# A burst of gathers opens after six of eight landings, and three one-hot tables are gathered from the second block on

## What is computed

```python
e = jnp.stack([tbl_0[ids[:, 0]], ..., tbl_25[ids[:, 25]]], axis=1)      # (2048, 26, 128)
combined = jnp.concatenate([sparse_x, dense_x[:, None, :]], axis=1)     # 27 features
interact = jnp.einsum('bfd,bgd->bfg', combined, combined)
z = interact[:, _TRIU_I, _TRIU_J]                                       # 351 pairs
h = jnp.concatenate([z, r_dense_x], axis=1)
h = jnp.maximum(h @ W_top1 + b_top1, 0.0)                               # 479 -> 512
h = jnp.maximum(h @ W_top2 + b_top2, 0.0)                               # 512 -> 256
y = h @ W_top3                                                          # 256 -> 1
```

## Time and profile before

| | us |
|---|---|
| median of 3 runs | 430.12 |
| lowest, highest | 429.4, 431.53 |
| span of the profiled execution | 427.9 |
| PE busy | 405.9 (95%) |
| POOL busy | 274.3 (64%) |
| ACT busy | 264.6 (62%) |
| DVE busy | 207.0 (48%) |

### The profile page before, as it was taken

One profiled execution on the slowest core, in us unless ns is written; L12 is line 12 of the kernel. 1 busy time (PEld: TensorE's weight loads), 2 busy tenths in 40 slices (PEclk: granted clock), 3 DMA queues, 4 the chain that ended last, 5 costly groups with the idle time before them and its releaser, 6 DMA issues.

```text
span 427.9 us, 8390 instructions
## 1 busy us (share of the span) xinstructions
PE 405.9 (95%) x3220; PEld 380.9 (89%) x3220; DVE 207.0 (48%) x238; ACT 264.6 (62%) x926; POOL 274.3 (64%) x292
## 2 busy tenths in 40 slices
PE   3898999999999989998999989999999989999997
PEld 2787899899999979998999989998899989989886
DVE  5788868441467134751367224661348324621142
ACT  3343477867675657657575756756576665766642
POOL 6557877766777667767776677766777676666000
PEclk9999999999999999999999999999999999999999
DMA  6776333312112121213112121212112121111000
GB/s 179 221 223 182 88 108 98 100 50 87 51 51 74 51 82 49 75 51 87 50 51 75 48 84 51 74 44 87 49 51 75 51 86 50 49 47 51 12 3 2
DMA packets 18073, 32.06 MB, mean 75 GB/s; under 512 B 5928, under 2 KB 8880, under 8 KB 18032
## 3 DMA queue, kind: packets, MB, share of 16 engines
q0 software_dynamic: 9088, 18.63, 15.6%
q1 hardware_dynamic: 8064, 12.08, 9.1%
q10 hardware_dynamic: 880, 0.80, 0.6%
HBM read 31.48 MB, written 0.01 MB: 74 GB/s over the span
## 4 chain that ended last, share of the span: by engine, by line
PE 82%; ACT 8%; DMA 7%; DVE 1%; issue 1%; ACTq 0%; SPq 0%
PE x_ps L612 29%; PE gram_ps L628 26%; PE tail_ps L683 12%; DMA hot_in<-in_tbl 7%; PE x_ps L593 6%; ACT gram L410 4%; PE tail_ps L660 3%; PE tail_ps L652 3%; PE tail_ps L689 2%; ACT h_hi L443 1%; ACT h L444 1%; ACT xt L386 1%; PE x_ps L720 1%; DVE onehot L873 0%; PE tail_ps L731 0%
## 5 line engine op out<-in xcount | busy, mean ns | idle before, releaser
L576 POOL DMA_INDIRECT raw<-in_tbl,ids_sb x284 | 273.4, 963 | 121.6 <-issue 74.0
L873 DVE TENSOR_TENSOR onehot<-ids_wide,row_ps 128x1024 fp32r<-128x1024 int16 (+1 forms) x142 | 163.6, 1181 | 103.7 <-PE x_ps L612 101.8
L410 ACT COPY gram<-gram_ps 32x104 f32<-32x104 f32 x496 | 117.4, 237 | 49.9 <-PE gram_ps L628 43.4
L612 PE MATMUL x_ps<-onehot,hot_hi 128*128 128x256 f32 x496 | 130.7, 298 | 10.0 <-ACT xt L386 9.6
L628 PE MATMUL gram_ps<-xt 128*128 128x108 f32 x1024 | 129.3, 276 | 2.1 <-ACT xt L820 0.8
L628 PEld LDWEIGHTS gram_ps<-xt 128*128 128x128 f32 x1024 | 122.1, 191 | 5.3 <-ACT gram L410 1.3
L612 PE MATMUL x_ps<-onehot,hot_lo 128*128 128x256 f32 x496 | 122.6, 281 | 0.0
L612 PEld LDWEIGHTS x_ps<-onehot,hot_hi 128*128 128x128 f32 x496 | 93.5, 188 | 15.8 <-ACT xt L386 11.4
L612 PEld LDWEIGHTS x_ps<-onehot,hot_lo 128*128 128x128 f32 x496 | 93.6, 189 | 0.0
L386 ACT COPY xt<-x_ps 128x128 f32<-128x128 f32 (+1 forms) x90 | 40.8, 509 | 42.7 <-PE x_ps L612 42.3
L820 ACT COPY xt<-x_ps 128x512 f32<-128x512 f32 (+1 forms) x78 | 44.2, 622 | 1.3 <-PE x_ps L593 1.3
(11 more groups left out here) (76 smaller groups left out, 317.0 us busy)
## 6 DMA issues: line engine op xcount, KB each, us to landing
raw<-in_tbl,ids_sb POOLq DMA_INDIRECT x284, 2.5
ids_wide<-in_hot_ids SPq DMA_DIRECT2D x16, 256.0 KB, 3.4
hot_in<-in_tbl SPq DMA_DIRECT2D x14, 256.0 KB, 3.3
hot_in<-in_tbl SPq DMA_DIRECT2D x6, 320.0 KB, 3.5
weights_in_place<-in_w SPq DMA_DIRECT2D x10, 128.0 KB, 2.2
dense_sb<-in_dense_t ACTq DMA_DIRECT2D x6, 128.0 KB, 2.4
dense_sb<-in_dense_t SPq DMA_DIRECT2D x2, 128.0 KB, 3.7
w1d_sb<-in_w SPq DMA_DIRECT2D x2, 128.0 KB
```

The source lines that it names most:

```text
L410: last = copy(gram[rows, :, per_fill * i:per_fill * (i + 1)], src)
L576: nc.gpsimd.indirect_dma_start(out=raw[k][:, f, :], out_offset=None, in_=sources[f], in_offset=bass.IndirectOffsetOnAxis(ap=ids_sb[:, t, f ...
L612: last = nc.tensor.matmul(ps, table[:, chunk_at[j] + c, :], moving[:, c - a, :], start=(c == 0 and table is tables_of[0]), stop=(c == chun ...
L873: nc.vector.tensor_tensor(columns(p), ids_wide[:, it // IDS % IDS_RING, it % IDS, 0:width].unsqueeze(1).to_broadcast([P, n, width]), row_n ...
```

## The change

`SHARES` becomes 3 from block 1 on, so that `MOST` is 3: the three tables of 10 chunks are all gathered there, and the seven tables of 8 chunks stay items. `raw` and `ids_sb` grow by one feature. The turns of a later tile take 19 gathers, still in five groups (3, 4, 4, 4, 4 in place of 3, 4, 3, 4, 4). Through `block_orders` the direct tables of block 0 become the items 0, 2, 4, 6, 7, 8 and 9 in place of 0, 2, 4, 6, 8 and 9. `BURST_OPEN = 2`: the wait ahead of a burst leaves out the last two gathers of the burst before, and both count on `last_in`.

```diff
-SHARES = (0, 2, 2, 2, 2, 2, 2, 2)
+SHARES = (0, 3, 3, 3, 3, 3, 3, 3)
 MOST = max(SHARES)
@@
 BURST = 8
+BURST_OPEN = 2
@@
     def is_last(t, f):
-        return gather_no[t, f] % BURST == BURST - 1
+        return gather_no[t, f] % BURST >= BURST - BURST_OPEN
@@
         def burst_landed(eng, k):
 
-            last_of = {(t, group_of[t, f]): f for t, f in gathers[k * BURST:(k + 1) * BURST - 1]}
+            last_of = {(t, group_of[t, f]): f for t, f in gathers[k * BURST:(k + 1) * BURST - BURST_OPEN]}
             for (t, g), f in last_of.items():
                 eng.wait_ge(lead_in[t % RAW][g], landed(t, g, False, f))
```

## The result

The changed kernel takes 417.0 us (median of 4 runs, 415.3 to 417.31) against 430.82 for the kernel before beside it (429.4 to 432.33): a ratio of 0.9656 (95% interval 0.9621 to 0.969). It is faster, by 3.1 to 3.8%. The forecast was 414.8. The profiled execution spans 415.5 us, where the prediction had 412.6.

What follows compares the result with a forecast made beforehand. PE bounds, POOL just under it: 427.9 - 16.45 - 0.45 + 1.4 = 412.4 us, a few tenths for their meeting give 412.6 profiled; the median, 2.2 above, is 414.8. Range 412 to 421.

Steps and rivals of the forecast that it cites:

- The burst's wait: POOL, every eighth gather: the wait of 0.70 us goes, 34.0 us in all, of which 3.5 and 1.0 stay.
- The second rival: POOL's bursts: the pause was needed, landings grow later and the wait returns whole; 439.1 us, median 441; chance 0.06.
- The price of a gather: POOL: fourteen added gathers at 1.25 us each cost 17.5 us; the last gather starts at 382.7.
- An item's products: PE, blocks 1 to 7: a dropped item saves 2.34 + 0.27 us each, two added transposes cost 0.26.
- The tail's cover: PE-ACT handoffs in a block's tail, 18 slots for 20: 0.2 us a block, 1.4 in all, 5.6 at worst.
- Block 0: PE's start: direct item 7 costs 2.0 us more but skips rounding and residue, ending at 36.75, saving 0.45 us.
- The two meet: At the end, POOL's last landing (385.9) and PE's due time (386.3) nearly coincide; a few tenths added for their meeting.
- the first rival: POOL takes over as bound, each burst keeping 0.1 to 0.2 us: 415.4 to 418.8, median 417.6 to 421; chance 0.15.
- the third rival: PE keeps more stalls, tail handoffs 5.6 us and item 7 held by its bank 1.1: 418.1, median 420; chance 0.13.

Runs made afterwards that it cites:

- three tables alone: The changed kernel with the old burst wait (seven of eight landings, BURST_OPEN = 1): 447.42 us, ratio 1.0385.
- opens after five: The changed kernel with a burst opened after five of eight landings (BURST_OPEN = 3): ratio 0.9669, 414.3 us in the profile.
- opened after five but for the first burst: The changed kernel with bursts opened after five of eight landings, except the first, which waits for seven: ratio 0.9666, 414.3 us in the profile.

## Why the prediction was right, and what it missed

The direction, the mechanism and the size held: 3.4% measured, 3.6% forecast (414.8 of 430.12 us), and 417.0 is inside the range, at the upper edge of what the forecast itself was given (412 to 417). Some of that is luck, since errors of both signs stand behind it. Point by point:

- **The burst's wait.** Right. With 0.55 us to spare the wait of 0.70 disappears at all but a few bursts; what was left, 5.7 us in total with 0.30 in each of 13 not a wait, is 1.8 us by that list, where the sum had 4.5. Landings under an unbroken stream did not grow: 2.6 us from issue in the median, 2.5 before. The second rival, the pause that was needed, is refuted by that; but its price was real, and too low. It had 439.1 us, with 0.70 for each burst. But 0.70 is the usual wait, and the mean behind block 0 of the kernel before is (34.0 - 6.85)/32 = 0.85. Summed from POOL's waits as they were, three tables with the old wait were expected at 443 us, and took 445.3.
- **The price of a gather.** Right: 1.25 us each. The last one starts at 383.62 for 382.7, with three tables alone at 415.3 for 413.6, with four tables at 396.64 for 397.9. Behind the first of these stand errors that partly cancel: gathers were to get shorter by 1.1 us in all, and got longer by 1.1 (287.7 us of them for 273.4, with fourteen more at 0.94), while all idle time between gathers, the 0.30 of the added ones aside, fell by 30.5 us (121.6 to 95.3, and 4.2) for 29.5. What lengthened them stands in the last section.
- **An item's products.** Right. Between the first turns of tiles 3 and 5 the products by tables took 16.19 us before and 13.57 in the kernel without the third gather, 2.62 less, where the sum had 2.34 + 0.27. (This is PEld again, each record up to the start of the next.) The transposes of `raw` took 3.99 for 3.38 by the same count, 0.61 more for 0.26, but the two added ones are not what was undersized: without the idle time behind them the rise is 0.24. The rest is mostly waits for ACT's copy, because two turns, seven transposes, now stand together where one of three stood before. PEld in the changed kernel:

```profile
215.97 0.79 PEld L594 LDWEIGHTS x_ps<-ident,raw 128*128 128x128 f32 x7
217.07 0.19 PEld L613 LDWEIGHTS x_ps<-onehot,hot_hi 128*128 128x128 f32 x1 [0.31 <-ACT xt L387]
```

- **The tail's cover.** This step was mis-sized, though a steady block hides it. The transposes of pairs rose by 0.56 us a block (1.26 to 1.82), more than half of it the wait for DVE above. The row I priced it by, ACT behind h1, was not the place: h1 even fell, 4.91 to 4.59, and no wait of PEld for ACT is left in it. A second error covered it: the stall behind two turns and the held item, which I said would stay at 1.38, fell to 0.92 in the blocks that have it, as the next timeline row of PE in the changed kernel shows. So steady blocks saved 2.2 to 2.3 us with the forecast's 2.15, but block 1 and the stretch behind it (from the first turn of tile 3 to that of tile 5), where that stall didn't stand, saved 1.9 and 1.6. Behind the last turn it takes 415.49 - 389.14 = 26.35 us for 26.1, which were not to change. In all PE saved 390.9 - 376.6 = 14.3 us from block 0's turn on, where the sum had 15.05.

```profile
243.09 0.39 PE L613 MATMUL x_ps<-onehot,hot_hi 128*128 128x256 f32 x1 [0.92 <-ACT xt L387]
```

- **Block 0.** Right in mechanism: the 2.0 us that item 7 costs more as a direct item are hidden by the rounding and residue that it no longer waits for. The saving of 0.45 us was oversized: it set the end of the last product before (37.20) against a start (36.75). From start to start it is 37.03 against 36.75, and the nine profiles with three tables average 37.1, no saving at all. Two profiles stand at 36.74 and 36.76, the others with three tables between 36.4 and 37.8. The 37.34 of the profile shown lies inside that spread, and two profiles of the same kernel are 0.58 apart; I take it for the varying arrival of the table loads, which no run isolates.
- **The two meet.** The forecast took the later of two nearly equal times and added 0.2 us. It should have added more: 1.2 us by the profile that opens after five, 1.6 by that without the third gathers. The profiles agree on this, but no median shows it: on one chip the changed kernel took 416.95 us, and 416.9 when it opened after five but for the first burst. The due times were compared at one point, the end, with 0.4 us between them; but each tile has its own due time, and the tight ones are the last turns of the even tiles. Where nothing waits (opening after five) the last gather of tile 14 starts at 356.65, 5.1 us before its turn (the last four of the twelve transposes shown), and that of tile 15 at 380.37, 7.3 us before:

```profile
356.65 0.94 POOL L577 DMA_INDIRECT raw<-in_tbl,ids_sb  x1 [0.31 <-issue]
360.90 1.51 PE L594 MATMUL x_ps<-ident,raw 128*128 128x128 f32 x12
```

  A gather that lands late at an even tile is never made up, because the stream in front of PE has no slack left.

  The 3.2 us from a gather's start to its landing were mis-read too. They run to POOL's next start; in the second profile of the changed kernel, where PE waits for a gather, it begins 2.7 us after that gather's start (360.21 and 362.91). In the profile shown it was 3.56 us at tile 14 (359.70 and 363.26) and 4.17 at tile 10, since these two gathers took 3.4 and 4.1 us to land where the median is 2.6; at tile 10 a load of `ids_wide` was under way. Tile 15, where I compared, had 2.9 us to spare in the end (its last gather landed at 386.2, and its turn came at 389.14).
- **The parts add up.** The profile is 3.1 us above the 412.4 that PE's sum gave: 0.75 in block 0 (37.34 for 37.03, where 0.45 were to be saved), 0.75 in PE's own saving, 1.6 at the meetings. Of this the forecast had 0.2.
- **The rivals.** POOL has not taken over with three tables: without its burden the block is the same 47.14 us. With four it has. The profile of 415.5 us does lie where the first rival put it (415.4 to 418.8), but not for its reason. PE's extra stalls exist, in the tail as the third rival said, but between PE and DVE: 1.8 us in all, where it had 5.6 behind ACT.

## What to carry to other kernels

Where two engines stream in lockstep, compare the pace of each, not the busy shares: POOL's 64% was 48.2 of 49.4 us once the time between its instructions and at its bursts was counted. Shifting work from one such stream to the other pays only to the point where both are equal, and needs the receiver's waits out of the way first; here each half of the change alone was worth nothing or -3.9%, and the pair +3.4%. When the slack is gone, price each due time, and leave the feeding stream a microsecond or two of lead (worth about 1 us in the profiles here, and not visible in the medians). And a schedule spread by proportion moves every handoff when the number of slots changes: look for two steps that fall together.

## What the runs showed of the hardware

**A long wait of PE can cost more than itself.** In the kernel with four tables PE waits 3.77 us for a gather at tile 14. The windows around it (first us and length, then PE, PEld, DVE, ACT and POOL busy, the granted clock, DMA), and the timeline behind it:

```profile
370.00:374.20 4.20, 0.52 (x5) 0.28 (x3) 0.00 (x0) 1.02 (x3) 2.98 (x5) 0.95 0.18 47
374.30:376.30 2.00, 2.00 (x10) 2.00 (x11) 0.00 (x0) 0.59 (x1) 1.69 (x2) 0.50 0.24 66
380.00:384.00 4.00, 3.74 (x33) 3.26 (x32) 0.42 (x1) 3.38 (x14) 2.90 (x4) 1.00 0.18 49
```
```profile
374.29 1.09 PE L594 MATMUL x_ps<-ident,raw 128*128 128x128 f32 x4 [3.77 <-DMA raw<-in_tbl,ids_sb]
...
375.60 0.41 PE L613 MATMUL x_ps<-onehot,hot_hi 128*128 128x256 f32 x1
375.81 0.41 PE L613 MATMUL x_ps<-onehot,hot_lo 128*128 128x256 f32 x1
...
377.60 0.28 PE L613 MATMUL x_ps<-onehot,hot_lo 128*128 128x256 f32 x1
377.71 0.28 PE L613 MATMUL x_ps<-onehot,hot_hi 128*128 128x256 f32 x1
```

PE sat idle, and the granted clock then was 0.50 (the 1.2 GHz level): products came 0.21 us apart; at 377.60 they come 0.11 apart again. With three tables and the old wait the same follows the wait of 5.2 us (clock 0.50 from 133 to 135 us). Behind the 0.81 us wait of the changed kernel the clock stayed at 1.00. Most of these slower stretches cost nothing in the end, since PE then waits for POOL again. The last one does: it follows a wait of 2.16 us at tile 14 (clock 0.51 from 391.6 to 394.0 us), and from that turn to the end three tables alone take 445.33 - 391.59 = 53.7 us, the changed kernel 415.49 - 363.26 = 52.2 and the kernel with the old wait in three bursts 419.69 - 367.47 = 52.2, both at a clock of 1.00. These 1.5 us of lower clock are a term that the sum for three tables alone, 2.3 us too low, did not have.

**DVE lengthens gathers.** The prediction leaned on the Trainium skill, SBUF — State Buffer, section "Who interferes with whom", for gathers held by a subtraction with two SBUF inputs. The changed kernel shows it, in agreement with that rule, at a place I had not listed, the residues of the weights (0.69 us each). The timeline of DVE, then that of POOL:

```profile
74.23 0.69 DVE L899 TENSOR_TENSOR weights_lo<-weights_in_place,weights_hi 105x512 fp32r<-105x512 f32 x1
...
89.78 0.69 DVE L899 TENSOR_TENSOR weights_lo<-weights_in_place,weights_hi 128x512 fp32r<-128x512 f32 x1 [2.47 <-ACT weights_hi L832]
```
```profile
74.48 1.25 POOL L577 DMA_INDIRECT raw<-in_tbl,ids_sb  x1 [0.30 <-issue]
...
89.82 1.46 POOL L577 DMA_INDIRECT raw<-in_tbl,ids_sb  x1 [0.30 <-issue]
```

An undisturbed gather takes 0.94. Four of the five residues meet a gather that is then 0.3 to 0.5 us longer, 1.8 us in all. For an engine without slack that is now a cost. That the residue holds the gather is read from their overlap; no run moves it away.
